# One step later: where a pair's convolution begins in a hand-ordered audio-tower kernel

## The chip, the cores and the metric

The kernel runs on one core of one Trainium2 chip. The metric is the device time of one launch in microseconds; smaller is better. The engines are named as in the profile: PE is TensorE (PEld its weight loads), DVE is VectorE, ACT is ScalarE, POOL is GpSimd, SP is SyncE.

## What is computed

The input is 16 batches of 375 rows of 128 channels. Two layers follow one another, cut here to their steps:

```
h = token mixer(x):  per row a softmax over 31 taps for each of 4 heads, weighted sum of neighbours,
                     conv1d 128 -> 512 channels, 31 taps, VALID (345 rows remain), selu, linear 512 -> 128
h = h + attention(layernorm(h)):   8 heads of 64, relative positions, softmax over 345 keys
h = h + mixture(layernorm(h)):     8 experts of 256, top 2, and a shared gated expert
h = h + linear attention(layernorm(h)):  8 heads of 16
h = h + mixture(layernorm(h)):     64 experts of 64, grouped top 8, capacity 256
```

## The kernel before

**Iterations.** The program is written out over iterations b = 0 to 16. In iteration b one core works on several batches at once: the attention of batch b, the first mixture of batch b-1, the late part (linear attention, second router) of batch b-2, the sending of rows of batch b-3 to a table in DRAM (POOL), and the token mixer's tap weights of batches b+4 and b+5. After the iterations, the 64 experts run over the table.

**The convolution** works on pairs of batches: pair k is batches 2k and 2k+1. It uses a fast form with nine products (`PRODUCTS`) in five groups (`GROUPS`: products 0 and 1, 2 and 3, 4, 5 and 6, 7 and 8) for each of four blocks of 128 output channels (o = 0 to 3). One pair costs `len(WORK)` = 852 matmuls of 128 x 174 in f16. The nine products' filters are read from DRAM through a ring of six buffers (ACT's queue issues the loads, `load_filters`, when a product is finished). Each group's sums lie in one of two PSUM banks, in turn, and have to be taken out before the bank's next group.

**Points.** An iteration is divided into POINTS = 46 points, at which a slice of the convolution may be put between other work: F0 to F2 at its front, P0 to P14 (one for each projection of `PROJ`: q, k and v), and s0 to s27 (`STEPS`). At step s (s < 24, `UNITS`) the attention's scores of unit s are made. The order on each engine in a step is fixed by the program:

- PE: scores S(s) into a bank of W; a piece of `late`; the transposes T(s-1) of the softmax's result; `hidden` (a first mixture's hidden matmuls, three for each half) at the steps of `FULL.hid`; at step `W2_STEP` = 20 of an odd iteration the last linear of the mixer (`tok_out`, 24 calls); then the convolution's slice of this point (`conv_at`); then, at s = 7, 13, 19, 25, the attention's outputs (`attend_pair`); then `down` (an expert's 6 calls, 12 matmuls in the trace) at the steps of `FULL.down` = 3, 6, 8, 11, 14, 16, 19, 22, 25.
- DVE: the maximum over S(s) (L1986); a piece of `late`; `tok_softmax`; `mixed` (adding an expert's output, L1921); the convolution's events of this point; the hidden product (L1905); `tok_out` of steps 20 and 21; and, at s = 9, 15, 21, 27, the attention's scaling (L2013).
- ACT: the exponential with that maximum (L1491); the copy of the transposes (L1497); the tanh of the hidden matmuls (L1458); the convolution's events of this point.

Five banks W0 to W4 are given out in an order made ahead of time (`place`, `w_uses`): PE waits before each use until the use before it has been read (`FREED`). The bank of `down` at step 22 was used last by S(22), so it waits for the exponential of step 22. The bank of the first hidden matmul of step 15 was used last by the one of step 14.

**The convolution's plan.** `Plan` spreads the 852 matmuls of a pair over the points from `HEAD` points ahead of the end of an odd iteration, through the whole even iteration that follows, to step 17 (`TAIL_STEP`) of the odd iteration after it. `PAIR_WEIGHTS` gives each point a weight (what is left of 3.3 us in a step, 24 for F0, 7 for a P point), so slices differ much. Where a group ends, it fixes at which later point its events run: 

```
ACT_EVENTS = {"e": (0, 1), "selu": (4, 2)}
DVE_EVENTS = {"U": (1, 1), "U1": (2, 1), "z02": (3, 1), "z13": (4, 1), "add": (4, 3)}
```

So "selu" (three activations on ACT, L1433, L1436, L1437) stands two points after the end of group 4 of its block, and "add" (one long DVE operation, L1680, which waits for them) three points after it. "e", "U", "U1", "z02" and "z13" take the groups' sums out of PSUM (L1427, L1692 and L1694, L1696, L1699, L1701). Pair 0 is convolved before the iterations. Pair 1 has a plan of its own (`SECOND`) that has no matmuls at the `HEAD` points and gives the same slices at the same places for either value. Pairs 2 to 7 use `STEADY`; pair k begins at the end of iteration 2k-3, fills iteration 2k-2 and ends in iteration 2k-1. So there are six odd iterations with a beginning pair at their end (1, 3, ..., 11); iterations 13, 14 and 15 have none.

Between step 17 and step 20 of an odd iteration the kernel takes the last pair's sums out and makes the next pair's input (`seq_round` on ACT at s17, `phases_split` on DVE at s18 and s19).

Of the kernel before, what the change touches and what calls it, by code (L numbers as in the profile page):

```python
# [77 lines left out]
STEPS = UNITS + 4  # L78
POINTS = FRONT + len(PROJ) + STEPS

HEAD = 7
TAIL_STEP = 17


# [28 lines left out]
def step_load(s):  # L113

    t = 0.63 * (s < UNITS) + 0.32 * (1 <= s <= UNITS) + 2.5 * (pair_at(s, 2) is not None) + 1.36 * (s in FULL.down)
    return t + (0.45 if FULL.hid.get(s, NHID) < 2 * E0 else 0.9 if s in FULL.hid else 0)
# [4 lines left out]
weight_of = [24, 4, 4] + [7] * len(PROJ) + [max(2, (STEP_US - step_load(s)) / CONV_US) for s in range(STEPS)]  # L121
PAIR_WEIGHTS = weight_of[POINTS - HEAD:] + weight_of + weight_of[:FRONT + len(PROJ) + TAIL_STEP]

# [35 lines left out]
lone_weights = [12, 2, 2] + [8] * len(PROJ) + [max(2, (STEP_US - lone_step(s)) / CONV_US) for s in range(STEPS)]  # L159
SECOND = Plan([0] * HEAD + lone_weights + weight_of[:FRONT + len(PROJ) + TAIL_STEP])  # L160

# [10 lines left out]
def conv_points(parity, at):  # L172

    out = []
    if parity == 0:
        out.append((0, HEAD + at))
    else:
        out.append((0, HEAD + POINTS + at))
        if at >= POINTS - HEAD:
            out.append((1, at - (POINTS - HEAD)))  # L180
    return out
# [2059 lines left out]
```

## Time and profile before

| what | value |
|---|---|
| median of 3 runs | 2299.24 us (2298.69 to 2302.49) |
| the profiled execution, own time | 2305.26 us |
| its span, first to last instruction | 2303.4 us |
| mean granted TensorE clock | 0.939 |
| busy: PE, PEld, DVE, ACT, POOL | 1959.6, 1579.7, 1457.8, 863.2, 741.2 us |

The busy time of an engine is a sum over the whole span. In the profile's 40 slices PE is at nine tenths or more from the fifth slice to the twenty-ninth, where the iterations run; the last quarter of the span (the 64 experts) is bound by other things. A row of the timeline gives start, duration, engine, line, operation, output<-inputs, shape and how many were merged; in square brackets stands how long the engine had been idle before it and for whom it waited. `W<-area_k,qv 128*115` is a scores matmul S (two for each step), `W<-ident,area_h` are the transposes T, `W<-mx_hl,w_hl` the hidden matmuls, `W<-w2eT,area_h` is `down`, `Cb<-seq_hi,ring` and `Cb<-seq_lo,ring` are the convolution, `Cb<-w2T,selu` is `tok_out`.

### The profile page before, as it was taken

Reading aid. Unit: us, or ns where it says so; the run is one execution under the profiler, and the core shown is the slowest. Engines: PE = TensorE matmul, PEld = TensorE weight load, DVE = VectorE, ACT = ScalarE, POOL = GpSimd, SP = SyncE. Lnnn points to the kernel's source line nnn. Section 1 sums busy time; section 2 is a strip of 40 time slices with the busy share of each in tenths; the row PEclk is TensorE's granted clock in tenths of the full one; section 3 lists DMA queues with packets and bytes.
Section 4 is the critical chain, followed back from the end, with each engine's and each line's share of the span. In section 5 each row is a group of like instructions: output and inputs, shape, how many; then the busy total and the mean of one; then the engine's idle time right before and its main releaser. Section 6 shows DMA issues by size and latency. Waiting matters only on the chain. (4 is left out here: it accounts for less than half of the span.)

```text
span 2303.4 us, 46715 instructions
## 1 busy us (share of the span) xinstructions
PE 1959.6 (85%) x16960; PEld 1579.7 (69%) x16960; DVE 1457.8 (63%) x4386; ACT 863.2 (37%) x2193; POOL 741.2 (32%) x630
## 2 busy tenths in 40 slices
PE   3688999999999999999999999999988887266660
PEld 2677887888788788878887888788776565133440
DVE  4784465677677766776676766666666668344440
ACT  2453454444344434443434443434334341021120
POOL 1000000013132322323232323232325235768885
PEclk9999999999999999999999999999999899577775
DMA  6874744434344333423342424133200001057665
GB/s 213 277 265 135 252 160 146 144 121 130 93 125 126 111 105 109 124 86 115 94 129 68 121 83 127 50 117 93 80 2 10 6 4 25 8 108 126 115 92 72
DMA packets 167588, 251.52 MB, mean 109 GB/s; under 512 B 67379, under 2 KB 123011, under 8 KB 166608
## 3 DMA queue, kind: packets, MB, share of 16 engines
q10 hardware_dynamic: 43672, 153.59, 20.6%
q0 software_dynamic: 56688, 51.20, 10.4%
q1 hardware_dynamic: 67016, 43.91, 7.3%
q8 instruction: 133, 2.18, 0.4%
q14 instruction: 79, 0.65, 0.1%
HBM read 203.09 MB, written 87.40 MB: 126 GB/s over the span
## 5 line engine op out<-in xcount | busy, mean ns | idle before, releaser
L997 PE MATMUL Cb<-seq_hi,ring 128*128 128x174 f16 x4544 | 599.9, 240 | 20.9 <-DVE seq_lo L1669 10.7
L997 PE MATMUL Cb<-seq_lo,ring 128*128 128x174 f16 x2272 | 528.9, 240 | 0.0
L913 POOL DMA_INDIRECT slots_dram<-rows,slot_i x384 | 454.5, 1184 | 121.1 <-issue 121.1
L997 PEld LDWEIGHTS Cb<-seq_hi,ring 128*128 128x128 f16 x4544 | 405.2, 98 | 52.1 <-DVE seq_lo L1669 11.3
L1491 ACT ACTIVATE area_h<-W,nmax 115x345 f32<-115x345 f32 x384 | 210.3, 548 | 578.9 <-DVE nmax L1986 576.7
L997 PE MATMUL W<-area_k,qv 128*115 128x345 f32 (+1 forms) x1536 | 418.4, 462 | 4.1 <-ACT area_h L1491 2.4
L901 POOL TENSOR_TENSOR rstd<-ve,minus_half 115x3 f32<-115x3 f32 x64 | 59.1, 923 | 1103.4 <-DVE ve L1735 556.9
L1986 DVE TENSOR_REDUCE nmax<-W 115x1 f32<-115x345 f32 x384 | 196.7, 513 | 211.6 <-PE W L997 180.2
L997 PEld LDWEIGHTS Cb<-seq_lo,ring 128*128 128x128 f16 x2272 | 222.0, 98 | 16.5 <-issue 1.3
L1170 PEld LDWEIGHTS W<-ident,area_h 115*115 115x115 f32 x1152 | 165.5, 180 | 94.9 <-ACT area_h L1491 41.2
L1905 DVE SCALAR_TENSOR_TENSOR area_h<-area_h,W 128x345 f32<-128x345 f32 x256 | 131.6, 515 | 147.8 <-ACT area_h L1458 117.8
L997 PE MATMUL W<-w2eT,area_h 128*115 128x128 f32 x1536 | 193.9, 276 | 24.9 <-ACT area_h L1491 17.7
L997 PEld LDWEIGHTS W<-area_k,qv 128*115 128x115 f32 (+1 forms) x1536 | 159.1, 157 | 63.8 <-issue 11.9
L1170 PE MATMUL W<-ident,area_h 115*115 115x115 f32 x1152 | 182.9, 267 | 22.5 <-ACT area_h L1491 21.2
L997 PEld LDWEIGHTS W<-w2eT,area_h 128*115 128x115 f32 x1536 | 175.5, 179 | 35.6 <-issue 23.9
L997 PE MATMUL W<-mx_hl,w_hl 128*128 128x345 f16 x960 | 190.3, 313 | 5.2 <-DVE area_h L1905 3.7
L1497 ACT ACTIVATE area_k<-W 115x345 f32<-115x345 f32 x384 | 173.2, 451 | 12.0 <-PE W L1170 11.5
L1466 ACT ACTIVATE qv<-W,q_b 128x345 f32<-128x345 f32 x128 | 70.1, 549 | 231.9 <-PE W L997 231.7
L1458 ACT ACTIVATE area_h<-W 128x345 f32<-128x345 f32 x288 | 132.2, 459 | 21.4 <-DVE area_h L1905 13.6
L997 PE MATMUL W<-area_x,w_hl 128*128 128x345 f16 x576 | 118.7, 321 | 2.2 <-DVE area_k L1965 1.6
L997 PEld LDWEIGHTS W<-mx_hl,w_hl 128*128 128x128 f16 x960 | 93.9, 100 | 30.7 <-DVE area_h L1905 8.0
L1921 DVE SCALAR_TENSOR_TENSOR h<-W,comb,h 115x128 f32<-115x128 f32 x384 | 109.9, 342 | 1.6 <-PE L L997 0.5
(243 smaller groups left out, 2883.6 us busy)
## 6 DMA issues: line engine op xcount, KB each, us to landing
ring<-filters_dram ACTq DMA_DIRECT2D x252, 512.0 KB, 3.5
filters_dram<-ring ACTq DMA_DIRECT2D x36, 512.0 KB, 4.5
slots_dram<-in_empty_slots POOLq DMA_DIRECT2D x8, 1544.0 KB, 13.6
area_k<-slots_dram SPq DMA_DIRECT2D x64, 193.0 KB
band<-band_dram SPq DMA_DIRECT2D x64, 189.0 KB, 2.9
slots_dram<-rows,slot_i POOLq DMA_INDIRECT x384
x_win<-in_xpad SPq DMA_DIRECT2D x16, 252.0 KB
qv<-in_wc POOLq DMA_DIRECT2D x2, 1984.0 KB, 10.9
```

Of the source, the lines that this page charges most:

```text
L901: pool.tensor_tensor(rstd[g][:, :], ve[g][:, :], minus_half[:, :], ALU.pow)\
L913: pool.indirect_dma_start(out=slots_d, out_offset=bass.IndirectOffsetOnAxis(ap=slot_i[parity(b)][:, m:m + 1], axis=0), in_=rows[parity(b)] ...
L997: return pe.matmul(o, l, r, start=start, stop=stop)
L1170: last = pe.transpose(w[0:A, i * A:(i + 1) * A], Pm[:, u % 2, i * A:(i + 1) * A], ident[0:A, 0:A])
L1458: act.activation(th[:, n % 2, :], bank[:, 0:TOK], ACT.Tanh, scale=0.5 / WS).then_inc(th_ready.h, 1)
L1466: act.activation(Q[:, h, :], bank[:, 0:TOK], ACT.Identity, bias=q_b[:, h:h + 1], scale=DH ** -0.5 / WS).then_inc(q_ready.h, 1)
L1491: act.activation(Pm[:, s % 2, :], bank[0:A, 0:TOK], ACT.Exp, bias=nmax[:, s % 2:s % 2 + 1], accum_out=psums[:, s // J, s % J:s % J + 1]).t ...
L1497: act.activation(pt_of(u), bank[0:A, 0:TOK].rearrange("p (i a) -> p i a", i=J), ACT.Copy)\
L1905: dve.scalar_tensor_tensor(dst, th[:, n % 2, :], 1.0, bank[:, 0:TOK], ALU.add, ALU.mult)\
L1921: ins = dve.scalar_tensor_tensor(dst[:, s], bank[0:A, s], scale, h1[:, s], ALU.mult, ALU.add)
L1986: dve.tensor_reduce(nmax[:, s % 2:s % 2 + 1], bank[0:A, 0:TOK], AX.X, ALU.max, negate=True).then_inc(nmax_ready.h, 1)
```

## The change

One constant:

```diff
-HEAD = 7
+HEAD = 6
 TAIL_STEP = 17
```

A pair's plan then starts at s22 of the odd iteration and not at s21, with one point fewer (81 and not 82). The plan's weights, the matmuls (852 for a pair) and their order stay, `W2_STEP` stays 20, and the plan of pair 1 keeps its places. Worked out from `Plan`, the slices (matmuls at each point) become, before -> after:

```
odd iteration, its end   s21 14->0  s22 1->2  s23 11->14  s24 22->30  s25 2->2  s26 46->24  s27 24->24
even iteration, F0-F2    13->18  2->3  2->3
  P0-P14                 4->5 4->5 4->4 4->5 4->5 3->5 4->5 4->4 | 6->5 7->5 6->5 7->4 6->5 7->4 6->5
  s0-s8                  18->22 13->14 13->13 4->4 19->17 15->25 5->8 1->2 8->13
  s9-s12                 24->12 17->12 4->5 21->20
  s13-s19                1->2 5->4 13->17 6->9 13->17 13->18 2->1
  s20-s27                24->19 20->16 2->1 15->12 31->22 2->1 24->25 23->24
odd iteration, F0-F2     13->22 2->3 2->4
  P0-P5                  4->6 4->7 4->6 5->5 5->5 4->5   (P6-P14: the same or one more)
  s0-s4                  as before;  s5 18->13  s6 5->3  s7 1->1  s8 9->7  s9 17->21  s10 17->21  s11 5->6
  s12-s16                as before
```

The events move with their groups: of block 0, "e" s25->s26, "U" s27->F0, "U1" F0->P0, "z02" P8->P10, "z13" s0->s1, "selu" s1->s2, "add" s2->s3; of block 1, "e" s4->s5, "U" stays at s9, "U1" s10->s11, "z02" s15->s16, "z13" s19->s20, "selu" s20->s21, "add" s21->s22; of block 2, "e" s23->s24, "U" s26->s27, "U1" s27->F0, "z02" P2->P3, the rest as before; of block 3 only "U1" s8->s9. The filter loads move with the products.

## Rows read from the trace of the kernel before

**Rows 1.** Busy time in three stretches; columns as in the head line.
```profile
core 0: us, PE busy (x) PEld busy (x) DVE busy (x) ACT busy (x) POOL busy (x), PEclk, DMA share, GB/s
191.20:1723.60 1532.40, 1487.64 (x13826) 1233.42 (x13824) 1043.53 (x3214) 655.72 (x1719) 373.39 (x335) 1.00 0.37 114
1699.00:1714.00 15.00, 13.08 (x101) 11.00 (x101) 7.55 (x27) 4.22 (x13) 0.00 (x0) 1.00 0.01 2
1723.80:1727.00 3.20, 3.20 (x15) 3.20 (x16) 1.44 (x3) 0.00 (x0) 0.00 (x0) 0.50 0.02 5
```

**Rows 2.** PE's waits from 858 to 1082 us (iterations 6 and 7): total, times, longest.
```profile
PE W L997 <- ACT area_h L1491: 2.3, 3, 1.2
PE W L1170 <- ACT area_h L1491: 1.7, 2, 1.5
PE L L1107 <- DVE lg L1630: 0.8, 1, 0.8
PE W L997 <- DVE area_h L1905: 0.6, 2, 0.4
```

**Rows 3.** PE, iteration 7: S(21), first convolution matmul of s21, S(22), `down`.
```profile
1038.50 0.74 PE L997 MATMUL W<-area_k,qv 128*115 128x345 f32 x2
...
1039.83 0.24 PE L997 MATMUL Cb<-seq_hi,ring 128*128 128x174 f16 x1
...
1040.89 0.77 PE L997 MATMUL W<-area_k,qv 128*115 128x345 f32 x2
...
1044.08 1.54 PE L997 MATMUL W<-w2eT,area_h 128*115 128x128 f32 x12 [1.16 <-ACT area_h L1491]
```

**Rows 4.** DVE and ACT, the same steps: hidden product, maximum 22, exponentials 21, 22.
```profile
1041.35 0.51 DVE L1905 SCALAR_TENSOR_TENSOR area_h<-area_h,W 128x345 f32<-128x345 f32 x1 [1.55 <-ACT area_h L1458]
...
1042.67 0.51 DVE L1986 TENSOR_REDUCE nmax<-W 115x1 f32<-115x345 f32 x1
...
1039.91 0.55 ACT L1491 ACTIVATE area_h<-W,nmax 115x345 f32<-115x345 f32 x1 [5.14 <-DVE nmax L1986]
...
1043.29 0.55 ACT L1491 ACTIVATE area_h<-W,nmax 115x345 f32<-115x345 f32 x1 [2.04 <-DVE nmax L1986]
```

**Rows 5.** PE, iteration 13, no convolution at these steps: S(21) and `down`.
```profile
1706.16 0.74 PE L997 MATMUL W<-area_k,qv 128*115 128x345 f32 x2
...
1711.73 1.54 PE L997 MATMUL W<-w2eT,area_h 128*115 128x128 f32 x12 [1.54 <-ACT area_h L1491]
```

**Rows 6.** PE, iteration 6: S(20), S(21), `down` of step 22.
```profile
921.54 0.74 PE L997 MATMUL W<-area_k,qv 128*115 128x345 f32 x2
...
924.25 0.77 PE L997 MATMUL W<-area_k,qv 128*115 128x345 f32 x2
...
929.87 1.54 PE L997 MATMUL W<-w2eT,area_h 128*115 128x128 f32 x12 [0.64 <-ACT area_h L1491]
```

**Rows 7.** ACT, iteration 6: "selu" begins, exponential 21, tanh, exponential 22.
```profile
923.83 0.87 ACT L1433 ACTIVATE conv_s<-conv_s,conv_nb 128x696 f32<-128x696 f32 x1
...
926.19 0.53 ACT L1491 ACTIVATE area_h<-W,nmax 115x345 f32<-115x345 f32 x1
...
927.06 0.45 ACT L1458 ACTIVATE area_h<-W 128x345 f32<-128x345 f32 x1
929.08 0.55 ACT L1491 ACTIVATE area_h<-W,nmax 115x345 f32<-115x345 f32 x1 [1.58 <-DVE nmax L1986]
```

**Rows 8.** PE and DVE, iteration 6: S(9), late transposes, `down` of s11; hidden product of s10.
```profile
886.54 0.74 PE L997 MATMUL W<-area_k,qv 128*115 128x345 f32 x2
...
892.93 0.46 PE L1136 MATMUL L<-ident,rows 115*128 115x115 f32 x3
...
894.28 1.50 PE L997 MATMUL W<-w2eT,area_h 128*115 128x128 f32 x12
...
892.78 0.51 DVE L1905 SCALAR_TENSOR_TENSOR area_h<-area_h,W 128x345 f32<-128x345 f32 x1 [0.46 <-ACT area_h L1458]
```

**Rows 9.** PE, front of iteration 13: transposes of the second norm after P5.
```profile
1625.48 0.52 PE L1157 MATMUL W<-ident,xh 115*128 115x115 f32 x3 [1.49 <-DVE xh L1745]
```

## The prediction

> **What bounds the kernel now.** I read the busy time by stretch first. Over the 1532.4 us of the iterations PE is busy for 1487.6 us, 97%, at a granted clock of 1.00, while DVE has 1043.5 and ACT 655.7 [rows 1]. The reader is to see that PE's instruction stream is the length of this stage. The change neither adds nor removes a matmul, so it can move the time only through PE's waits. The second view is therefore the list of waits for one pair (iterations 6 and 7): four kinds and 5.4 us in all out of 224 us [rows 2]. No row names a filter load, so the ring of six is far enough ahead, and six buffers stay six when the loads move with the products. The third view is the timeline of PE, ACT and DVE around each wait: what was put between the start of the chain that PE waits for and the wait. A convolution matmul that stands there costs nothing, because PE would stand still instead. One that stands elsewhere costs its pitch. From the first one of s21 to S(22), 14 of them take 1040.89 - 1039.83 = 1.06 us, so 0.076 us each [rows 3].
>
> **Part 1: the end of the odd iteration.** In iteration 7 `down` of step 22 starts 1044.08 - 1038.50 = 5.58 us after S(21), and PE has waited 1.16 us for the exponential of step 22 [rows 3]. The chain to it does not pass through the convolution: exponential 21 at 1039.91, then tanh, hidden product 1041.35, maximum 22 at 1042.67, exponential 22 at 1043.29 [rows 4]. Between S(21) and `down` stand 14 + 1 convolution matmuls, 15 x 0.076 = 1.14 us. Iteration 13 has none there and is the same otherwise: from S(21) to `down` it takes 1711.73 - 1706.16 = 5.57 us [rows 5]. So all 15 are free today. After the change two are left (s22). The other 13 have to run elsewhere: 13 x 0.076 = 0.99 us lost in each of the six odd iterations in which a pair begins, 5.9 us. The bounds: 0 if they find another wait to fill, 0.99 if not. I take 0.99, since PE has no wait from s23 to s27, where 14 + 30 + 2 + 24 + 24 now stand.
>
> **Part 2: steps 20 to 22 of the even iteration.** Before: `down` of step 22 starts 929.87 - 921.54 = 8.33 us after S(20), past 24 + 20 + 2 = 46 convolution matmuls, with a wait of 0.64 us [rows 6]. "selu" stands on ACT in step 20 and takes 926.19 - 923.83 = 2.36 us until the exponential of step 21 can start behind it [rows 7]. After: 19 + 16 + 1 = 36 matmuls, and "selu" stands in step 21 behind the tanh and ahead of exponential 22, for which PE waits. Counted from S(20): S(21) at 924.25 - 921.54 - 5 x 0.076 = 2.33 [rows 6]; exponential 21 follows S(21) by 1039.91 - 1038.50 = 1.41 where ACT is free [rows 3, 4], so 3.74; tanh 927.06 - 926.19 = 0.87 later, 4.61, for 0.45; "selu" from 5.06 to 7.42; exponential 22 then, and `down` 929.87 - 929.08 = 0.79 behind it [rows 6, 7], at 8.21. That is 0.12 earlier than today, with 10 matmuls (0.76 us) fewer behind it: a loss of 0.64 us. The other bound is the chain without "selu" in its way: exponential 22 comes 1043.29 - 1039.91 = 3.38 after exponential 21 in iteration 7 [rows 4], which puts `down` at 3.74 + 3.38 + 0.79 = 7.91 at the latest, 0.42 earlier than today, a loss of 0.34. "add" (DVE, pitch about 1.3 us) leaves the place ahead of the hidden product of step 21, which is why this chain is short. I take 0.64: ACT works in the program's order, and exponential 21 today starts exactly when "selu" is over.
>
> **Part 3: steps 9 to 11 of the even iteration.** Slices fall from 24 + 17 + 4 = 45 to 12 + 12 + 5 = 29. Today there is no wait here. But "U" of block 1 stays in step 9 on DVE, and behind it stand the maximum of step 10, the norm of the late part, for whose result the transposes at 892.93 are made, and the hidden product 892.78, which ends at 893.29 and which `down` of s11 (894.28) needs [rows 8]. That chain starts with S(9) at 886.54 and ends 6.75 us later, `down` can start at about 6.9, and does today at 7.74. It can move up by 0.84 us at most while 16 x 0.076 = 1.22 leave: a loss of 0.38 us. The bounds are 0 (the chain moves up too) and 0.38; I take 0.38. At step 15 the first hidden matmul waits for the one of step 14 (part of the 0.6 us that PE waits for L1905 [rows 2]) and step 14 has one matmul less: 0.08 us.
>
> **Part 4: everything else.** More matmuls at F0 to P6, s0, s5, s8 and s15 to s18 cost their pitch and hide no wait. The events that move by one point cost nothing while PE has work: "U1" at P0 sits in front of the k projections on DVE, where the more PE work ahead of them (5 matmuls, 0.38 us) covers it; "selu" of block 0 at s2 now delays the exponential of s3 and no longer that of s2. Without PE's work over them, each would be its own length, 0.5 to 2.4 us for each pair. The late transposes of odd s1 wait 0.8 us for L1630 [rows 2]; the slices and events from P11 to s1 stay, so this wait stays. One thing is won: at the fronts of iterations 12 and 13 the transposes after P5 wait for the norm (1.49 us in 13 [rows 9]), and there the slices from F1 to P5 grow by 8 and by 11. In 13 this hides 11 x 0.076 = 0.83 us. In 12 about 0.1 is left, since "U1" at P0 lengthens the DVE chain by some 0.5. Together -0.9 us.
>
> **Sum.** Odd ends 6 x 0.99 = 5.9; even iterations 2 to 12, 6 x (0.64 + 0.38 + 0.08) = 6.6; iterations 12 and 13 -0.9: +11.6 us. The profiled execution took 2305.26 us, its span 2303.4; the sum gives 2316.9 for it. That execution lies 6.0 us above the median of the runs shown, so for the median 2299.24 + 11.6 = 2310.8. The last quarter of the span (the experts) starts after the iterations and shifts as a whole.
>
> **The rivals.** All times are of the median.
>
> A, my forecast: both the odd ends and the even iterations lose, 2307 to 2314. Chance 0.62.
>
> B, only the odd ends lose. For it: there the trace has its own control, iteration 13. The even parts rest on chains that I put together from pieces, and "add" leaving the chain to `down` of step 22 could give back what the thinner slices take. 5.9 - 0.9 = +5.0, so 2304.2. Chance 0.16.
>
> C, no difference: the 13 matmuls of each odd end find waits elsewhere (0.8 us at odd s1, those at P5). Against it: the odd s1 wait depends on the order of P12 to s0, which stays. Within 4.6 us of before, 2299. Chance 0.10.
>
> D, faster. The mechanism is the even step 22: if the chain to exponential 22 becomes shorter by "add"'s whole 1.3 us (it held the hidden product at 927 us) and "selu" were not in front of it, `down` would come at S(20) + 7.0, 1.3 us earlier than today, for 0.76 us of matmuls fewer: 0.54 won in each pair, 3.2 us. It decides only if the odd ends lose less than that in all, that is if more than seven of the 13 matmuls fall into waits. With all of them it is 2299.2 - 3.2 - 0.9 = 2295. Chance 0.03.
>
> E, more than the forecast: a moved event lands on a chain I took as covered (the norm before P6, whose transposes today come with nearly no slack, or T(3) behind "selu" at s2), or the clock falls. Another 0.5 to 1 us in each pair, 2314 to 2317. Chance 0.09. About the clock: through the thin steps of iteration 13, 1699 to 1714 us, it is granted at 1.00, with PE busy for 13.08 of 15 us, and after the waits behind them it is at 0.50 for 3.2 us [rows 1], which is 1.2 GHz and would cost half of such a stretch, 1.6 us. The changed odd steps 19 to 22 look like the first of these two stretches. (The Trainium skill, "TensorE: Matmul & The Clock Gate", section "Why this matters for your kernels", warns that idle gaps between bursts of matmuls bring the clock back to its lower level. Going by that rule alone, each of the six odd ends could cost those 1.6 us, 2320 in all; going by the row of iteration 13, whose gap is 1.54 us at clock 1.00, nothing. By that row the longer wait in front of `down` stays harmless.)
>
> **Range and chances.** From B's value to E's lower edge: 2303 to 2315 leaves out C and D, 0.13, and about half of E. This kernel's measurement tells 0.2%, 4.6 us, from no change. Slower by more: A, E and most of B (0.13 of its 0.16, since it sits at +5.0, just beyond), 0.84. Within 0.2%: C and the rest of B, 0.13. Faster: 0.03.
>
> **What would show it.** In the profile after: at the six odd ends `down` of step 22 starts 5.6 us after S(21), as now, with a wait of about 2 us before it. In the even iterations ACT shows "selu" (L1433) behind the tanh of step 21, exponential 22 right behind it, and PE a wait of about 1.4 us in front of `down`. DVE's hidden product of s10 still comes 6.2 us after S(9), and short waits appear before the late transposes and `down` of s11. One pair of iterations is 2.1 us longer than its 224 us. PE's waits for one pair grow from 5.4 to about 7.5 us. The forecast is wrong if `down` in an odd step 22 moves up with the missing matmuls, if "selu" does not hold exponential 22, or if a wait appears that is not in this list.

## The result: 11 us slower, and the profile after

| | before | after |
|---|---|---|
| median of 8 runs each | 2302.16 us (2298.69 to 2305.82) | 2313.16 us (2310.09 to 2323.92) |
| ratio, 95% interval | | 1.0052 [1.0042, 1.0063] |
| profiled execution, its own time | 2305.26 us | 2310.09 us |
| its span, granted clock | 2303.4 us, 0.939 | 2308.3 us, 0.940 |
| S(0) of iteration 1 to S(0) of iteration 14 | 1443.3 us | 1453.2 us |
| first instruction to S(0) of iteration 0 | 207.5 us | 202.8 us |

The kernel is 0.5% slower. The two profiled executions differ by 4.8 us only, because the part before iteration 0, which the change doesn't touch, took 4.7 us less in the second. The iterations themselves grew by 9.9 us, and that is what the views below are about. S(0) of iteration 6 stands at 856.31 us in the kernel after, S(0) of iteration 8 at 1082.58. The windows view of this pair, the columns as in [rows 1]:

```profile
core 0: us, PE busy (x) PEld busy (x) DVE busy (x) ACT busy (x) POOL busy (x), PEclk, DMA share, GB/s
856.31:1082.58 226.27, 219.36 (x2041) 181.94 (x2040) 160.88 (x501) 95.87 (x252) 66.14 (x59) 1.00 0.35 108
```

The same view of the kernel before, over its own pair of iterations:

```profile
858.32:1082.59 224.27, 218.86 (x2041) 182.02 (x2040) 160.72 (x501) 96.11 (x252) 65.48 (x59) 1.00 0.37 109
```

The number of instructions is the same on each engine, the clock too, and the pair is 226.27 - 224.27 = 2.00 us longer. The prediction said 2.1. It is the pair that grew most: counted in the same way, the pairs from iteration 2 on grew by 1.58, 1.86, 2.00, 1.90, 1.95 and 1.36 us.

**The odd end.** The timeline of PE in iteration 7 of the kernel after, for [rows 3]:

```profile
1039.21 0.74 PE L997 MATMUL W<-area_k,qv 128*115 128x345 f32 x2
...
1040.54 0.74 PE L997 MATMUL W<-area_k,qv 128*115 128x345 f32 x2
1041.41 0.53 PE L1170 MATMUL W<-ident,area_h 115*115 115x115 f32 x3
1041.77 0.61 PE L997 MATMUL W<-mx_hl,w_hl 128*128 128x345 f16 x3
1042.63 0.62 PE L997 MATMUL W<-mx_hl,w_hl 128*128 128x345 f16 x3 [0.25 <-DVE area_h L1905]
1043.08 0.24 PE L997 MATMUL Cb<-seq_hi,ring 128*128 128x174 f16 x1
1043.16 0.24 PE L997 MATMUL Cb<-seq_lo,ring 128*128 128x174 f16 x1
1044.79 1.43 PE L997 MATMUL W<-w2eT,area_h 128*115 128x128 f32 x11 [1.39 <-ACT area_h L1491]
```

and of DVE and ACT, for [rows 4]:

```profile
1040.63 0.55 ACT L1491 ACTIVATE area_h<-W,nmax 115x345 f32<-115x345 f32 x1 [5.14 <-DVE nmax L1986]
...
1044.01 0.55 ACT L1491 ACTIVATE area_h<-W,nmax 115x345 f32<-115x345 f32 x1 [2.04 <-DVE nmax L1986]
...
1042.06 0.51 DVE L1905 SCALAR_TENSOR_TENSOR area_h<-area_h,W 128x345 f32<-128x345 f32 x1 [1.55 <-ACT area_h L1458]
```

S(22) comes 1.33 us after S(21), where it came 2.39 after it in [rows 3], and still `down` starts 1044.79 - 1039.21 = 5.58 us after S(21), to the hundredth as before. The exponentials are 3.38 us apart in both kernels. The slice was thinned, the chain beside it was not. Note that the wait written at `down` grew only from 1.16 to 1.39. Most of the rest of the 0.99 us stands at the transposes (0.87 us after S(22), where it was 0.60) and at the second three hidden matmuls (0.86 us after the first three, where it was 0.45; the bracket shows only 0.25 of that).

**The even steps 20 to 22.** PE in iteration 6, for [rows 6]:

```profile
921.12 0.74 PE L997 MATMUL W<-area_k,qv 128*115 128x345 f32 x2
...
923.45 0.77 PE L997 MATMUL W<-area_k,qv 128*115 128x345 f32 x2
...
929.34 1.54 PE L997 MATMUL W<-w2eT,area_h 128*115 128x128 f32 x12 [1.30 <-ACT area_h L1491]
```

ACT there, for [rows 7]:

```profile
924.99 0.55 ACT L1491 ACTIVATE area_h<-W,nmax 115x345 f32<-115x345 f32 x1 [1.47 <-DVE nmax L1986]
...
925.87 0.46 ACT L1458 ACTIVATE area_h<-W 128x345 f32<-128x345 f32 x1
926.21 0.88 ACT L1433 ACTIVATE conv_s<-conv_s,conv_nb 128x696 f32<-128x696 f32 x1
927.12 0.88 ACT L1436 ACTIVATE conv_s<-conv_s,conv_ba 128x696 f32<-128x696 f32 x1
927.90 0.77 ACT L1437 ACTIVATE conv_s<-conv_s 128x696 f32<-128x696 f32 x1
...
928.58 0.53 ACT L1491 ACTIVATE area_h<-W,nmax 115x345 f32<-115x345 f32 x1
```

"selu" (L1433, L1436, L1437) stands between the tanh and exponential 22, which has no wait of its own: it starts when "selu" lets ACT go. `down` comes 929.34 - 921.12 = 8.22 us after S(20).

**The even steps 9 to 11.** PE of the kernel after, for [rows 8]; S(9), S(11), the late transposes, T(10), `down`:

```profile
886.16 0.74 PE L997 MATMUL W<-area_k,qv 128*115 128x345 f32 x2
...
890.67 0.77 PE L997 MATMUL W<-area_k,qv 128*115 128x345 f32 x2
891.56 0.51 PE L1136 MATMUL L<-ident,rows 115*128 115x115 f32 x3
891.91 0.47 PE L1170 MATMUL W<-ident,area_h 115*115 115x115 f32 x3
...
893.04 1.50 PE L997 MATMUL W<-w2eT,area_h 128*115 128x128 f32 x12
```

No row of PE has a bracket here, and yet the late transposes come 0.89 us after S(11) and not 0.60, as in the trace before (S(11) at 892.33, the transposes at 892.93 [rows 8]). The reason stands on PE's other row, the weight loads of the same stretch:

```profile
891.56 0.30 PEld L1136 LDWEIGHTS L<-ident,rows 115*128 115x128 f32 x3 [0.69 <-DVE rows L1745]
```

The transposes take their data as weights, and the load waits for the norm's rows (L1745) from DVE.

**The list of PE's waits** for this pair in the kernel after, for [rows 2]:

```profile
PE W L997 <- ACT area_h L1491: 3.7, 3, 1.4
PE W L1170 <- ACT area_h L1491: 1.7, 2, 1.5
PE L L1107 <- DVE lg L1630: 0.7, 1, 0.7
PE W L997 <- DVE area_h L1905: 0.2, 1, 0.2
```

6.3 us, against 5.4: the list grew by 0.9 us where the pair grew by 2.0. It counts the matmuls' waits alone. What a weight load waits is not in it, and a bracket can show less than the distance grew, as at the hidden matmuls above.

### The profile page after: what moved, and what is told of

The parts are those of the page before. It is cut to its first block and busy times, and to the rows that moved or that the text cites. A ratio compares the mean times of both kernels' runs of the same rounds, so it can differ in the third digit from the quotient of the medians.

```text
span 2308.3 us, 46750 instructions
## 1 busy us (share of the span) xinstructions
PE 1960.6 (85%) x16960; PEld 1577.3 (68%) x16960; DVE 1457.8 (63%) x4386; ACT 861.9 (37%) x2193; POOL 743.8 (32%) x630
## 5 line engine op out<-in xcount | busy, mean ns | idle before, releaser
L997 PE MATMUL Cb<-seq_hi,ring 128*128 128x174 f16 x4544 | 596.7, 240 | 19.5 <-DVE seq_lo L1669 10.7
L997 PE MATMUL Cb<-seq_lo,ring 128*128 128x174 f16 x2272 | 527.4, 239 | 0.0
L997 PEld LDWEIGHTS Cb<-seq_hi,ring 128*128 128x128 f16 x4544 | 404.5, 97 | 50.0 <-DVE seq_lo L1669 11.3
L1491 ACT ACTIVATE area_h<-W,nmax 115x345 f32<-115x345 f32 x384 | 210.3, 548 | 585.3 <-DVE nmax L1986 582.7
L997 PE MATMUL W<-area_k,qv 128*115 128x345 f32 (+1 forms) x1536 | 418.3, 462 | 4.2 <-ACT area_h L1491 2.4
L997 PEld LDWEIGHTS Cb<-seq_lo,ring 128*128 128x128 f16 x2272 | 221.5, 98 | 17.0 <-issue 0.2
L997 PE MATMUL W<-w2eT,area_h 128*115 128x128 f32 x1536 | 193.7, 276 | 30.8 <-ACT area_h L1491 23.5
L997 PEld LDWEIGHTS W<-w2eT,area_h 128*115 128x115 f32 x1536 | 175.5, 179 | 41.1 <-issue 29.7
L997 PEld LDWEIGHTS W<-area_k,qv 128*115 128x115 f32 (+1 forms) x1536 | 159.4, 157 | 63.9 <-issue 11.1
L997 PE MATMUL W<-mx_hl,w_hl 128*128 128x345 f16 x960 | 191.3, 313 | 6.7 <-DVE area_h L1905 4.4
L997 PE MATMUL W<-area_x,w_hl 128*128 128x345 f16 x576 | 118.5, 321 | 1.6 <-DVE area_k L1965 1.6
L997 PEld LDWEIGHTS W<-mx_hl,w_hl 128*128 128x128 f16 x960 | 93.4, 100 | 33.7 <-DVE area_h L1905 11.6
```

The costliest lines, as they stand in the source:

```text
L997: return pe.matmul(o, l, r, start=start, stop=stop)
L1491: act.activation(Pm[:, s % 2, :], bank[0:A, 0:TOK], ACT.Exp, bias=nmax[:, s % 2:s % 2 + 1], accum_out=psums[:, s // J, s % J:s % J + 1]).t ...
```

## The experiments

All edits go through two small additions to `Plan`, shown once. `moves` adds matmuls to a point's slice or takes them away, counted from the pair's first point; `held` lets one event run later than its table says.

```diff
-    def __init__(self, weights):
+    def __init__(self, weights, moves=(), held={}):
+        self.held = held
...
+        for p, n in moves:
+            counts[p] += n
...
-... if self.group_at[(o, n)] + later == p]
+... if self.group_at[(o, n)] + later + self.held.get((name, o), 0) == p]
```

Two theories are told apart. The waits theory is the prediction's: a matmul put before a chain's end is free, elsewhere it costs its pitch. Its rivals: the loss comes from something else that the one point brings (the events, the fronts), or the even parts are no loss. In the edited kernels every line behind the edit stands three higher: L1491 is L1494 there, and L997 is L1000.

### The odd end alone, thin and full

Kernel before, slices of s21 to s24 from 14, 1, 11, 22 to 0, 2, 16, 30 (thin) and to 31, 1, 6, 10 (full).

```diff
-STEADY = Plan(PAIR_WEIGHTS)
+STEADY = Plan(PAIR_WEIGHTS, [(0, -14), (1, 1), (2, 5), (3, 8)], {})
```

> The kernel before (HEAD 7) with only the end of the odd iteration changed as the change does it: in STEADY the slices of s21 to s24 are 0, 2, 16, 30 in place of 14, 1, 11, 22. The same 48 matmuls, every event and every slice from s25 on as before. Waits theory (what stands between S(21) and down of step 22 is free, the chain there does not move): 13 matmuls x 0.076 = 0.99 us lost in each of six odd iterations, +5.9 us, ratio about 1.0026; down starts 5.6 us after S(21) as before, its wait grows from 1.16 to about 2.2 us; the even iterations unchanged. Rival (the time comes from the later events and the thinner even slices, and the chain moves up when PE is earlier): +0 to +1 us, ratio 1.000.

```diff
-STEADY = Plan(PAIR_WEIGHTS)
+STEADY = Plan(PAIR_WEIGHTS, [(0, 17), (2, -5), (3, -12)], {})
```

> The kernel before (HEAD 7) with slices 31, 1, 6, 10 at s21 to s24 in place of 14, 1, 11, 22: 17 more matmuls in front of down of step 22. Waits theory: the wait of 1.16 to 1.32 us there is filled by 17 x 0.076 = 1.29 us of work, so -1.2 us in each of six odd iterations, -7 us, ratio about 0.997. S(22) starts 1.29 us later and must still not hold up its maximum, which starts 1.78 us after S(22) today and needs 0.8: so about 0.3 us of that may be given back, -5.5 to -7 us. Rival (the slices' places do not matter, only the total does): 1.000.

Measured: thin 1.0023 [1.0006, 1.0039], full 0.9981 [0.9968, 0.9994]; medians 2400.68 and 2388.38 us, before 2392.25 us (why this is 90 us more than above is a section of its own, below). With two matmuls between S(21) and `down` the interval is 5.58 us in every odd iteration, with 15 it is 5.58, and with 32 it is 5.90, the wait at `down` 0.18 us. The thin end alone, with no event moved and no other slice touched, costs time, and the prediction's part 1, 5.9 us or 1.0025, lies in the interval; that interval goes from 1.4 to 9.3 us, so the size rests on the trace. In the full one 17 more matmuls (1.29 us of pitch) lengthen the interval by 0.32 us: 0.97 us won in each of six, 5.8 us, for 4.5 measured (0.9981). Where the 0.32 comes from stands in iteration 7 of this kernel, PE's S(21), S(22) and `down`, and DVE's maximum 22:

```profile
1071.47 0.74 PE L1000 MATMUL W<-area_k,qv 128*115 128x345 f32 x2
...
1075.15 0.77 PE L1000 MATMUL W<-area_k,qv 128*115 128x345 f32 x2
1077.37 1.54 PE L1000 MATMUL W<-w2eT,area_h 128*115 128x128 f32 x12 [0.18 <-ACT area_h L1494]
...
1075.95 0.52 DVE L1989 TENSOR_REDUCE nmax<-W 115x1 f32<-115x345 f32 x1 [0.23 <-PE W L1000]
```

Maximum 22 now waits for S(22), which 31 matmuls have put 3.68 us behind S(21), and starts 4.48 us after S(21) where it started 4.17 after it [rows 3, 4]. So S(22) is itself a link of the chain, and only so much work is free ahead of it. The same 32 matmuls, put as 27 ahead of S(22) and 5 behind it, take 5.60 us (the last kernel of the table further down).

### Mending the changed kernel's odd end, and its step 11

Kernel after; s22 to s25 from 2, 14, 30, 2 to 30, 6, 10, 2:

```diff
-STEADY = Plan(PAIR_WEIGHTS)
+STEADY = Plan(PAIR_WEIGHTS, [(0, 28), (1, -8), (2, -20)], {})
```

> The kernel after (HEAD 6) with slices 30, 6, 10, 2 at s22 to s25 in place of 2, 14, 30, 2: 28 more matmuls in front of down of step 22, events as in the kernel after. Waits theory: the longer wait there (2.2 us) is filled by 28 x 0.076 = 2.1 us, -2.1 us in each of six odd iterations against the kernel after, -12.6 us; against the kernel before +11 - 12.6, so -1 to -2 us, ratio about 0.9995. Rival (a convolution that begins at s22 costs by its later place, events and filter loads): as the kernel after, 1.005.

Kernel after; s11 and s12 of the even iteration from 5, 20 to 10, 15:

```diff
-STEADY = Plan(PAIR_WEIGHTS)
+STEADY = Plan(PAIR_WEIGHTS, [(35, 5), (36, -5)], {})
```

> The kernel after (HEAD 6) with 10 and 15 matmuls at s11 and s12 of the even iteration in place of 5 and 20. Waits theory: the new wait at s11 (0.35 us, late transposes and down wait for a DVE chain from step 9) is for the larger part in front of the late transposes, ahead of this slice, but a start of down of s11 that is fixed by the hidden product of s10 lets 5 x 0.076 = 0.38 us in for nothing: 0.1 to 0.35 us in each of six even iterations, -0.6 to -2.1 us against the kernel after, ratio to the kernel before 1.0038 to 1.005. If the wait is wholly that of the late transposes: nothing, 1.005.

Measured on the same chip, beside the same runs of before as the two above: 0.9981 [0.9971, 0.9991] and 1.0024 [1.0012, 1.0035], medians 2387.62 and 2398.70 us. PE of iteration 7 of the first, S(21), the hidden matmuls of step 22, `down`:

```profile
1069.62 0.74 PE L1000 MATMUL W<-area_k,qv 128*115 128x345 f32 x2
...
1073.03 0.61 PE L1000 MATMUL W<-mx_hl,w_hl 128*128 128x345 f16 x3 [0.25 <-DVE area_h L1908]
...
1075.76 1.50 PE L1000 MATMUL W<-w2eT,area_h 128*115 128x128 f32 x12
```

The wait at `down` is gone: 28 more matmuls (2.12 us) in an interval longer by 6.14 - 5.58 = 0.56 us. That is 1.56 us in each of six, 9.4 in all, and not the 2.1 and 12.6 that were expected: the rest of what PE stands still there lies ahead of these matmuls, at the transposes and at the hidden matmuls (0.25 in the rows), where they can't fill it. The second kernel of this pair won nothing (below), and the two lie 11.1 us apart.

The second comes out at the lower end of its expectation. From S(9) to `down` of s11 it takes 7.27 us, against 6.89 in the kernel after: the five matmuls put into s11 cost all of their 0.38 us. They stand behind the late transposes, and the wait is ahead of those. So nothing is won at s11: by the trace, the work that could fill the wait of part 3 would have to stand ahead of the late transposes, in s9 and s10. No run put it there.

### "selu" out of the way of exponential 22

Kernel after, block 1's "selu" in step 22 and "add" in step 23; no slice changes.

```diff
-STEADY = Plan(PAIR_WEIGHTS)
+STEADY = Plan(PAIR_WEIGHTS, [], {('selu', 1): 1, ('add', 1): 1})
```

> The kernel after (HEAD 6) with selu of block 1 at s22 and add at s23 (one point later each), in STEADY; slices as in the kernel after. Waits theory: exponential 22 no longer stands behind selu, so down of step 22 starts about 2.33 + 1.41 + 2.92 + 0.79 = 7.45 us after S(20) in place of 8.22 (2.92 is 3.38 of iteration 7 less 0.46 for tok_out), with the same 36 matmuls: -0.77 us in each of six even iterations, -4.6 us against the kernel after, ratio to the kernel before about 1.003. Rival (not selu but the maximum of step 22 or the hidden product holds down): 0 to -0.3 us each, 1.005.

and with the odd end mended as well:

```diff
-STEADY = Plan(PAIR_WEIGHTS)
+STEADY = Plan(PAIR_WEIGHTS, [(0, 28), (1, -8), (2, -20)], {('selu', 1): 1, ('add', 1): 1})
```

> The kernel after with both: slices 30, 6, 10, 2 at s22 to s25 of the odd iteration, and selu and add of block 1 one point later. Waits theory: the run with the full s22 showed down 6.15 us after S(21) with 30 matmuls ahead of it (28 x 0.076 - 0.57 = 1.56 us won each), selu late 0.77 each; 6 x 2.33 = -14 us against the kernel after, ratio to the kernel before about 0.999 (if the two add up). Rival: they share a wait and do not add up, 1.001 or more.

and both in the kernel before, with slices 27, 5, 6, 10 at s21 to s24 and the two events two points later:

```diff
-STEADY = Plan(PAIR_WEIGHTS)
+STEADY = Plan(PAIR_WEIGHTS, [(0, 13), (1, 4), (2, -5), (3, -12)], {('selu', 1): 2, ('add', 1): 2})
```

> The kernel before (HEAD 7) with slices 27, 5, 6, 10 at s21 to s24 of the odd iteration, and selu and add of block 1 two points later (s22, s23). Waits theory: 32 matmuls in front of down of step 22 of the odd iteration, which still starts 5.6 us after S(21), so 17 x 0.076 = 1.29 us won each; in the even iteration down starts about 2.71 + 1.41 + 2.92 + 0.79 = 7.83 us after S(20) in place of 8.33, 0.5 us won each. 6 x 1.8 = -10.7 us, ratio to the kernel before about 0.9953. Rival: add at s23 delays the chain to step 24 and gives the 0.5 back, 0.9967.

with the kernel after, unchanged, run beside them:

> The kernel after itself, unchanged, timed beside the others of this group and against the kernel before on the same chip. Waits theory: 1.005 again, if this chip adds no waits of its own; on the chip of the first four runs, where from iteration 3 on every kernel has waits that the trace gives as issue or remote, the ratio was not measured for it.

| kernel | median | ratio to before (2368.47 us) | even S(20) to `down` | its wait | odd S(21) to `down` | its matmuls |
|---|---|---|---|---|---|---|
| after, unchanged | 2366.63 | 0.9994 [0.9980, 1.0007] | 8.22 | 1.30 | 5.57 | 2 |
| after, "selu" later | 2363.69 | 0.9979 [0.9964, 0.9994] | 7.57 | 0.64 | 5.57 | 2 |
| after, both | 2356.10 | 0.9940 [0.9918, 0.9962] | 7.57 | 0.64 | 6.15 | 30 |
| before, both | 2358.65 | 0.9953 [0.9935, 0.9971] | 7.89 | 0.21 | 5.60 | 32 |

ACT in iteration 6 of the third of these, exponential 21, tanh, exponential 22, then "selu" (its first activation, L1433 in the kernel after):

```profile
945.70 0.55 ACT L1494 ACTIVATE area_h<-W,nmax 115x345 f32<-115x345 f32 x1 [1.47 <-DVE nmax L1989]
...
946.58 0.46 ACT L1461 ACTIVATE area_h<-W 128x345 f32<-128x345 f32 x1
948.62 0.55 ACT L1494 ACTIVATE area_h<-W,nmax 115x345 f32<-115x345 f32 x1 [1.58 <-DVE nmax L1989]
...
949.83 0.88 ACT L1436 ACTIVATE conv_s<-conv_s,conv_nb 128x696 f32<-128x696 f32 x1
```

With "selu" behind it, exponential 22 waits for its maximum and comes 2.92 us after exponential 21, where it came 3.59 after it. The matmuls between are the same 36, so the interval's 0.65 us are won whole: 3.9 us for six (0.77 each and 4.6 were expected), and 2.9 measured between the medians, where the two ratios' intervals overlap; here too the trace carries the size. "add" was moved along, but it stands behind maximum 22 on DVE in the kernel after as well (928.81 and 927.28), so it is not what held exponential 22. That shows that ACT's order, and not the thin slices alone, makes `down` late in the kernel after. Both mends together win 10.5 us over the kernel after by the medians (13.3 by the intervals: 9.4 and 3.9). In the kernel before the same two hide 17 matmuls more in the odd end (1.27 us for six) and 0.44 us in the even one: 10.2 us by the intervals, 9.8 by the medians. So both versions beat both kernels, and the larger part of it has nothing to do with `HEAD`: the slices that stand ahead of a known wait were too thin from the start. Both were run in this measurement alone, which has the added waits of the next section. Without those, the intervals put the last kernel 10 us under before, and the third one, which has the change's own 11 us to make up, only 2: by that estimate the one to keep is the last. The measured times of the two, 2.6 us apart the other way, are too wide to choose by.

### Why the second measurement of the change shows nothing

The unchanged kernel after was 1.0052 at first and 0.9994 in the measurement above, while its three intervals were the same to 0.01 us. There the chip took 2368 us for the kernel before, not 2302. To see how much such a measurement can tell, the kernel before was run against itself, and the kernel after a third time.

> The kernel before, unchanged, timed against itself: ratio 1.000, and its width is what this measurement tells from no change. Its trace is wanted beside that of the kernel after on the same chip. Theory one (chips that add waits of their own take back the change's cost): if the chip adds such waits (issue or remote in the list, iterations 8 us longer from iteration 3 on), the sum of waits from 400 to 1720 us differs by less than 3 us between the two kernels, while down of step 22 starts 5.58 us (odd, after S(21)) and 8.33 us (even, after S(20)) as always. Theory two (the first comparison was off): the waits differ by 10 us here too.

> The kernel after, unchanged, beside the kernel before of the same group. On a chip without waits of its own: 1.005. On one with them: 0.999 to 1.001, and down of step 22 still at 5.58 us (odd, 2 matmuls ahead of it) and 8.22 us (even), so that the 10 us have to be given back at other places: fewer added waits near s1, s12 to s14 and P14 than in the kernel before, place by place.

Measured: 0.9986 [0.9974, 0.9999] and 0.9997 [0.9985, 1.0009], before again 2368 us. A kernel against itself is 0.14% off there, its interval just short of 1, so a ratio like the thin end's 1.0023 is not far beyond what such a measurement gives for no change. PE's waits of this second execution of the kernel before, 400 to 1720 us (total, times, longest), the first rows of the list that have no engine behind them:

```profile
PE W L1170 <- issue: 7.8, 9, 2.2
...
PE W L997 <- issue: 5.1, 9, 0.9
```

In the first trace of the kernel before no row of this list says "issue". The pair of iterations 6 and 7 takes 870.30 to 1106.16, 235.86 us, at the same clock of 1.00 (the windows view), with the same instructions:

```profile
870.00:1106.00 236.00, 221.88 (x2042) 182.10 (x2041) 161.12 (x501) 96.72 (x252) 66.96 (x59) 1.00 0.35 104
```

So PE does the same work and stands still for 235.86 - 224.27 = 11.6 us more. Compared step by step with the first trace of the same kernel, nearly all of the added time stands at the same steps: s1 to s4, s12 to s15, and between P13 and S(0). Over iterations 1 to 13 it is 56.3 us in this execution of the kernel before, and 51.4 and 52.2 us in two of the kernel after. By kind of iteration: in the even ones at s1 to s4 and s12 to s15 11.9 + 19.7 = 31.6 us for before, 21.9 and 22.8 for after; in the odd ones there 22.0 for before, 26.1 and 23.6 for after. So the kernel after has 9 to 10 us less added time in the even steps, 2 to 4 more in the odd ones, and 4 to 5 less in all. That is half of the change's 9.9 us. In these three executions S(0) of iteration 1 to S(0) of iteration 14 is still 5.0 and 5.8 us longer in the kernel after, while the medians lie 1 to 2 us the other way; the profiled execution of the kernel before, 2361.81 us, lies 6.5 us below the median of 2368.36. So how the whole difference goes is not known from three executions; the thinner slices and later events of block 0 stand near those steps. One more pair was to tell:

```diff
-STEADY = Plan(PAIR_WEIGHTS)
+STEADY = Plan(PAIR_WEIGHTS, [], {('z13', 0): 1, ('selu', 0): 1, ('add', 0): 1})
```

> The kernel before, with one thing of the change: of block 0, the events z13, selu and add stand one point later (s1, s2, s3 of the even iteration, as after the change; before s0, s1, s2). No slice changes. It asks where the change's ten microseconds go on the chips on which it measures as no difference: there the kernel after has some 4 us fewer of the added waits at s1 to s4 of the even iterations than the kernel before. Theory one (where the events stand sets how much of these added waits falls at s1 to s4): on such a chip faster by 2 to 5 us, ratio about 0.999, and the added waits at even s1 to s4 fall from about 12 us to about 8 us over iterations 2 to 13; on a chip without added waits no difference, 0.999 to 1.001. Theory two (the events have no part in it; slices or chance set them): no difference on either kind of chip, and about 12 us of added waits at even s1 to s4 where they occur. In both the interval from S(21) to the expert's last product of the odd step 22 stays 5.58 us and that from S(20) in the even step stays 8.33 us.

> The kernel after, unchanged, once more beside the kernel before. On a chip without added waits, as the first one, 1.005; on a chip with added waits at s1 to s4, s12 to s15 and at the start of iterations, 0.999 to 1.001. The theory that the first ratio was the chance of that one measurement expects 1.000 on either. The three intervals at the expert's last products are 5.58, 8.22 and 6.89 us in each case.

Measured: 0.9996 [0.9987, 1.0005] and 1.0047 [1.0033, 1.0060], before 2303.21 us. This measurement had next to no added waits, although it ran on the chip that had taken 2368 and 2392 us: PE's lists have no row with "issue", and the kernel after, with intervals of 5.58, 8.22 and 6.89 us, stands still longer than in its first trace at two places alone, 1.1 us at s19 of iteration 9 and 1.6 at s1 of iteration 13. So the first ratio was no accident: without the added waits the change costs 0.5%, twice measured. That "z13", "selu" and "add" of block 0 cost nothing clear of noise when they stand one point later is shown too, as part 4 of the prediction has it; its other moved events were not moved alone. Whether they matter to the added waits was not seen, since none occurred, and stays open.

## Why the prediction was right

**Part 1, right to the hundredth.** 13 matmuls, 0.99 us in each odd end: comparing the two traces step by step, with 0.0757 us for each matmul of difference, s22 of iterations 1, 3, 5, 7, 9 and 11 has 0.98 or 0.99 us more standing still, 5.9 in all. The thin end alone on the kernel before costs time too (1.0023, with 1.0025 for 5.9 us). What was wrong is the side remark "with a wait of about 2 us before it". The wait at `down` is 1.39, and the rest is spread over the transposes and the hidden matmuls ahead of it. "All 15 are free" is right, but not for any number of them: S(22) is a link of the chain too, as the full end shows.

**Part 2, right.** 0.64 us predicted, 0.65 found in each of six even iterations; `down` at 8.22 for 8.21, exponential 22 at 928.58 - 921.12 = 7.46 for 7.42, the wait 1.30 for 1.4. That it fits to 0.01 is luck in part: exponential 21 came 0.13 us later than the chain has it (924.99 - 921.12 = 3.87 for 3.74), and "selu" began 0.34 us after the tanh and not 0.45. The chain was put together from pieces of two iterations, and "selu" as its last link is shown by moving it.

**Part 3, right in size, its place not quite.** 0.35 or 0.36 us in iterations 4 to 12 for 0.38 predicted, and DVE's hidden product of s10 comes 6.13 us after S(9) for 6.2. In iteration 2 it is 0.16 at s11 and 0.14 at s9. The prediction named two things that could be late, the late transposes and `down`; it is the first, and so five matmuls at s11 won nothing. Its 6.9 us was worked out from the hidden product, which didn't hold `down`; that the norm's chain brings `down` to the same 6.89 is luck. The 0.08 at step 15 is there in five of the six, and iteration 6 has 0.24 less instead.

**Part 4.** Iterations 12 and 13 were the mis-sized term: 0.9 us predicted, 0.66 us found, all in 13. The transposes after P5 waited 1.49 us [rows 9] and now, in the timeline of PE of the kernel after:

```profile
1631.20 0.51 PE L1157 MATMUL W<-ident,xh 115*128 115x115 f32 x3 [0.83 <-DVE xh L1745]
```

Eleven more matmuls (0.83 us) hid 0.66. Small changes that the prediction had at nothing come to about -1.3 us in all: -0.08 us at each odd s1 (-0.2 in iteration 13), -0.3 at s3 of iteration 2, -0.5 between s23 of iteration 13 and S(0) of 14 (a stretch that takes 28.5 to 31.4 us in the traces of unchanged kernels), and once +0.45 at s19 of iteration 7.

**The sum.** Predicted 5.9 + 6.6 - 0.9 = 11.6; found in the iterations 5.9 (part 1) + 3.9 (part 2) + 2.2 (part 3) + 0.2 (step 15) - 0.7 (iteration 13) - 1.3 (the rest), which is 10.2, for 9.9 measured from S(0) to S(0) and 11.0 between the medians. 2310.8 us was said on the median of three runs of before, 2299.24; eight give 2302.16, and with that the sum would have said 2313.8, for 2313.16. So close a hit is luck: the 11.6 was 1.4 us over the sum found in the traces, and the ratio's interval alone goes from 9.7 to 14.5 us.

**The rivals.** B, that only the odd ends lose, is ruled out: the even intervals lose 0.65 and 0.35 us and the experiment with "selu" gives 0.65 back. C had the 13 matmuls fall into other waits: their whole 0.99 us is lost, and the wait at odd s1 shrank by 0.08 only. D had `down` at S(20) + 7.0: it came at 8.22, and at 7.57 with "selu" out of the way. (D's condition is miscounted: with a gain of 3.2 us it needs six of the 13 in waits, 7 x 0.076 x 6 = 3.2, and not more than seven.) E had the clock or a covered event: over 1042 to 1047 us, with PE busy for 3.36 of 5 us, the windows view of the kernel after shows a granted clock of 1.00, like iteration 13 before. (The Trainium skill, "TensorE: Matmul & The Clock Gate", section "Why this matters for your kernels", warns of idle gaps. The gaps in front of `down` are 1.39 us here and the longest of PE's waits from 400 to 1720 us is 2.0; from 191.2 to 1723.6 us the clock is granted at 1.00, so the 2320 us that E worked out by that rule did not come.)

## What to carry to other kernels

Before work is moved between slots of a stream that is nearly full, look for the slots that stand ahead of a wait: what is in them is free, and what leaves them is paid in full. The same rows show the gain: fill such a slot up to the chain's length (here 32 matmuls where 15 stood), but see which instructions of the full stream are links of the chain themselves, and put no more ahead of each than its slack (27 ahead of S(22) kept the interval at 5.60 us, 31 made it 5.90). Keep long operations of a second engine behind, not ahead of, the one that ends the chain. Read the length of the interval from a fixed start to the waiting instruction, not the wait printed beside it, which shows only a part.

## What the hardware showed that was not expected

**Added waits that come and go with the measurement.** The same kernel took 2302, 2392, 2368, 2368 and 2303 us in five measurements, the runs within each spread over 0.2 to 0.6%. The second, the third and the fifth ran on one chip, so they don't belong to a chip. In the traces of the kernel before of the first and the fourth, the clock in the iterations (1.00) and the pace of the matmuls (0.076 us) are the same, the DMA queues' shares within half a point; part of the added time stands as "issue" or "remote", at the steps named above for the most part. One place of the kernel with the full odd end, timeline of PE, SP and ACT in iteration 6: eight small matmuls into L, the two that wait for them, and PE's next:

```profile
990.40 0.37 PE L1000 MATMUL L<-area_b,x_win 126*32 126x96 f32 x8
...
992.78 0.34 SPq L771 DMA_DIRECT2D x_win<-in_xpad  x1
992.79 0.34 ACT L1391 ACTIVATE y<-L,tok_bias 128x96 f32<-128x96 f32 x1 [1.25 <-remote]
993.18 0.88 PEld L1000 LDWEIGHTS L<-wlT,x_T 128*96 128x96 f32 x8 [1.19 <-ACT y L1391]
```

The matmuls end at 990.77, and two engines that wait for them go on together 2.0 us later; PE then waits for one of these. By the profile the work is done and its readers start late. What delays them is not settled by these runs.

**How much it hides.** Where these waits occur, a change worth 0.5% measured as nothing, twice, while the mends inside one such measurement still differed from one another by what their intervals say (10.5 us for 13.3 and 9.8 for 10.2). A single time would have misled; the lengths of three intervals, the same to 0.02 us in iterations 6 and 7 of all four traces of the kernel after, did not.
